# Media attention with turns four groups behind the scores, and fixed parts of the eight banks

## What is computed

```python
def _L2_xattn_ref(x, media, media_mask, ...):
    qn = layernorm(x, ln_q_g, ln_q_b)
    q = qn @ Wq * scale
    k, v = jnp.split(media @ Wkv, 2, axis=-1)
    sim = jnp.einsum('bhid,bhjd->bhij', q, k)
    sim = jnp.where(media_mask[:, None, None, :], sim, neg_inf)
    attn = jax.nn.softmax(sim, axis=-1)
    out = jnp.einsum('bhij,bhjd->bhid', attn, v)
    x = x + jnp.tanh(attn_gate) * (out @ Wo)
    h = gelu(layernorm(x, ...) @ W1) @ W2
    return x + jnp.tanh(ff_gate) * h
```

## Time and profile before

| | us |
|---|---|
| median of 3 executions | 1693.32 (1692.87 to 1697.88) |
| the profiled execution | 1686.46 |
| its span, first to last instruction | 1684.4 |
| PE busy | 1552.4 (92%) |
| PE weight loads busy | 1339.0 (79%) |
| DVE busy | 967.5 (57%) |
| ACT busy | 668.8 (40%) |
| mean granted clock of PE | 0.968 of full speed |

### The profile page before, as it was taken

The page is one execution under the profiler, slowest core; times in us unless marked ns, Lnnn a source line. Parts: engine busy times, 40 slices in busy tenths (PEclk is TensorE's granted clock), DMA queues, the critical chain, the costliest instruction groups (busy, mean ns, idle before and its releaser), DMA issues.

```text
span 1684.4 us, 31094 instructions
## 1 busy us (share of the span) xinstructions
PE 1552.4 (92%) x11106; PEld 1339.0 (79%) x11106; DVE 967.5 (57%) x2163; ACT 668.8 (40%) x1773; POOL 246.7 (15%) x346
## 2 busy tenths in 40 slices
PE   5879899899899899999889999998999999899899
PEld 4747677667667679999778878887988878788799
DVE  2646655646646675676274646564655555647554
ACT  1314334434424462222454444443336353535332
POOL 0134324324324300000000000000100000000010
PEclk9989999999999889999999999999999999999999
DMA  3203000000000020000100000002000000000000
GB/s 144 69 13 107 4 1 3 3 0 3 3 0 1 1 82 1 0 0 1 53 5 4 3 3 3 1 1 82 0 33 25 4 3 3 3 0 1 1 25 26
DMA packets 13224, 30.20 MB, mean 18 GB/s; under 512 B 2400, under 2 KB 8800, under 8 KB 12512
## 3 DMA queue, kind: packets, MB, share of 16 engines
q1 hardware_dynamic: 13152, 29.23, 4.9%
HBM read 27.13 MB, written 2.10 MB: 17 GB/s over the span
## 4 chain that ended last, share of the span: by engine, by line
PE 77%; DVE 10%; issue 6%; ACT 3%; POOL 2%; DMA 0%; DVEq 0%; SPq 0%; ACTq 0%; POOLq 0%
PE bank L774 69%; PE bank L787 8%; DVE nmax L1258 2%; DVE pT L1157 2%; DVE stats L1187 1%; ACT p L1472 1%; DVE xn L1233 1%; POOL kbd L1652 1%; DVE xn L1237 1%; POOL rstd L1619 1%; DVE o_rounded L1342 0%; ACT hT L1423 0%; DVE aggr L1192 0%; DVE xn L1235 0%; DMA p<-in_media 0%
## 5 line engine op out<-in xcount | busy, mean ns | idle before, releaser
L1472 ACT ACTIVATE p<-bank,nmax 128x128 f32<-128x128 f32 x1024 | 285.4, 375 | 394.3 <-DVE nmax L1258 393.9
L774 PE MATMUL bank<-v,pT 128*128 128x65 f32 (+2 forms) x2048 | 258.1, 263 | 46.1 <-issue 25.0
L774 PEld LDWEIGHTS bank<-v,pT 128*128 128x128 f32 x2048 | 252.3, 194 | 54.0 <-issue 42.3
L1258 DVE TENSOR_REDUCE nmax<-bank 128x4 f32<-128x512 f32 x256 | 170.1, 686 | 161.7 <-PE bank L774 161.4
L774 PE MATMUL bank<-w_ff_rounded,hT_rounded 128*128 128x256 f32 x944 | 218.4, 287 | 0.8 <-DVE kbd L1320 0.8
L774 PE MATMUL bank<-kbd,hT 64*128 64x128 f32 (+1 forms) x1280 | 205.1, 342 | 5.0 <-ACT hT L1423 3.9
L787 PEld LDWEIGHTS bank<-consts,p 128*128 128x128 f32 x1040 | 125.4, 143 | 100.4 <-issue 79.5
L774 PE MATMUL bank<-xT_rounded,w_ff_rounded 128*128 128x256 f32 x864 | 196.8, 286 | 4.5 <-issue 3.0
L1157 DVE COPY pT<-bank 128x512 f32<-128x512 f32 x256 | 174.6, 682 | 34.8 <-PE bank L787 34.3
L774 PE MATMUL bank<-xn_rounded,w_ff_rounded 128*128 128x256 f32 x608 | 172.9, 284 | 0.0
L787 PE MATMUL bank<-consts,p 128*128 128x128 f32 x1040 | 161.6, 278 | 7.5 <-ACT p L1432 5.0
(11 more groups left out here) (147 smaller groups left out, 2798.8 us busy)
## 6 DMA issues: line engine op xcount, KB each, us to landing
ctxT<-in_ctxT SPq DMA_DIRECT2D x32, 128.0 KB, 2.4
w_ff<-in_w1b SPq DMA_DIRECT2D x6, 640.0 KB, 6.6
w_att<-in_w2a SPq DMA_DIRECT2D x1, 3072.0 KB, 10.6
w_att<-in_w3a SPq DMA_DIRECT2D x1, 3072.0 KB, 10.3
w_att<-in_w1a SPq DMA_DIRECT2D x1, 2432.0 KB, 12.3
hT<-in_xT SPq DMA_DIRECT2D x8, 256.0 KB, 3.1
o<-in_x SPq DMA_DIRECT2D x8, 256.0 KB, 3.1
w_ff<-in_w2b SPq DMA_DIRECT2D x1, 2048.0 KB, 7.4
```

The costliest lines, as they stand in the source:

```text
L774: return pe.matmul(dst, lhsT, rhs, start=first, stop=last)
L1258: dve.tensor_reduce(nmax[:, ph.place[s] % P_RING, :], bank[:, :].rearrange("p (h t) -> p h t", h=QUAD), AX_X, ALU.max, negate=True).then_i ...
L1472: t = act.activation(p_ring[i % P_RING][:, part], bank[:, part], ACT.Exp, bias=nmax[:, i % P_RING, j:j + 1])
```

## The change

In media attention the turn moves from two groups behind the scores to four, and the product from three to five. An iteration has 21 slots instead of 19. There are eight `p` buffers there instead of four; the new four lie in free columns of `kbd0` and `kbd1`. Banks are no longer dealt over all steps in phases 3 and 5: scores use banks 0 to 3 in turn, every `oT2` uses bank 7, and all other steps share banks 4 to 6 in turn. In `steps_attn2` unit A's four `oT2` go to slots 8, 9, 11 and 12, its `wo` to slot 15, B's `oT2` to slots 17 to 20, and the third `oT2_low` of B is put ahead of B's last `oT2`. No instruction that computes is added or removed. The other phases keep their order and banks. Lines of the changed kernel stand 3 to 18 lower: matmuls at L792, transposes at L805, DVE's maxima at L1276, its copy of a turn at L1175, its low part at L1360.

```diff
+MEDIA_RING = 8
+MEDIA_SKEW_T = 4
+MEDIA_SKEW_O = 5
...
-        if 0 <= i - SKEW_T < len(groups):
-            slot += here(("turn",) + groups[i - SKEW_T])
-        if 0 <= i - SKEW_O < len(groups):
-            slot += here(("values",) + groups[i - SKEW_O])
+        if 0 <= i - skew_t < len(groups):
+            slot += here(("turn",) + groups[i - skew_t])
+        if 0 <= i - skew_o < len(groups):
+            slot += here(("values",) + groups[i - skew_o])
...
-                 (a, n, n + SKEW_O),
-                 (low(A_), n + 1, n + SKEW_O + 1),
-                 (here(("wo", A_), ("end", A_)), n + SKEW_O + 2, n + SKEW_O + 2),
+                 (a, n, n + skew_o),
+                 (low(A_), n + 1, n + skew_o + 1),
+                 (here(("wo", A_), ("end", A_)), n + skew_o + 2, n + skew_o + 2),
...
+                 (low(B_)[2:3], end, end),
                  (b[3:], end, end),
                  (ahead(*pre[-2:]), end, end),
-                 (low(B_)[2:], end, end),
+                 (low(B_)[3:], end, end),
...
         self.bank = {s: i % BANKS for i, s in enumerate(jobs)}
+        if index in (3, 5):
+
+            of_scores = [s for s in jobs if s[0] == "scores"]
+            others = [s for s in jobs if s[0] not in ("scores", "oT2")]
+            self.bank = {s: i % QUAD for i, s in enumerate(of_scores)}
+            self.bank |= {s: QUAD + i % (QUAD - 1) for i, s in enumerate(others)}
+            self.bank |= {s: BANKS - 1 for s in jobs if s[0] == "oT2"}
...
+        p_media = [p[:, :] for p in p_ring] + [kbd[u][:, at:at + BANK] for at in (2304, 2816) for u in range(UNITS)]
```

More of the change, by code:

```diff
@@ L114, in ahead, with attention @@
     return [(s, 1) for s in steps]
-def attention(streams):
+def attention(streams, skew_t, skew_o):
     groups = [(kind, u, b, g) for kind, u in streams for b in range(ROWS) for g in range(GROUPS)]
     slots = []
-    for i in range(len(groups) + SKEW_O):
+    for i in range(len(groups) + skew_o):
         slot = []
@@ L201, in steps_self @@
     end = 4 * n + SKEW_O - 1
-    return weave(attention([("self", A_), ("self", B_), ("cross", A_), ("cross", B_)]),
+    return weave(attention([("self", A_), ("self", B_), ("cross", A_), ("cross", B_)], SKEW_T, SKEW_O),
                  (here(*pre_self(B_)[2:]), 0, n - 1),
@@ L240, in steps_attn2 @@
     n = ROWS * GROUPS
-    end = 2 * n + SKEW_O - 1
+    skew_o = MEDIA_SKEW_O
+    end = 2 * n + skew_o - 1
     a, b = (here(*[("oT2", u, b, j) for b in range(ROWS) for j in range(2)]) for u in range(UNITS))
-    return weave(attention([("media", A_), ("media", B_)]),
+    return weave(attention([("media", A_), ("media", B_)], MEDIA_SKEW_T, skew_o),
                  (here(*pre_attn2(B_)), 0, n - 2),
-                 (a, n, n + SKEW_O),
-                 (low(A_), n + 1, n + SKEW_O + 1),
-                 (here(("wo", A_), ("end", A_)), n + SKEW_O + 2, n + SKEW_O + 2),
+                 (a, n, n + skew_o),
+                 (low(A_), n + 1, n + skew_o + 1),
+                 (here(("wo", A_), ("end", A_)), n + skew_o + 2, n + skew_o + 2),
                  (ahead(*norms), n, n + 3),
@@ L250, in steps_attn2 @@
                  (low(B_)[0:2], end - 2, end - 1),
-                 (ahead(*pre[:-3]), n + SKEW_O + 1, end - 1),
+                 (ahead(*pre[:-3]), n + skew_o + 1, end - 1),
                  (ahead(*pre[-3:-2]), end, end),
+                 (low(B_)[2:3], end, end),
                  (b[3:], end, end),
                  (ahead(*pre[-2:]), end, end),
-                 (low(B_)[2:], end, end),
+                 (low(B_)[3:], end, end),
                  (here(("wo", B_), ("end", B_)), end, end))
@@ L459, in build @@
         pT_ring = [sb_twin(f"pT{i}", [P, BANK]) for i in range(PT_RING)]
-        nmax = sb("nmax", [P, P_RING, QUAD])
+        nmax = sb("nmax", [P, MEDIA_RING, QUAD])
         rinv = sb("rinv", [P, 2, QUAD])
@@ L574, in x_low, with ring @@
             return xn[u][:, c, 1, :]
+        p_media = [p[:, :] for p in p_ring] + [kbd[u][:, at:at + BANK] for at in (2304, 2816) for u in range(UNITS)]
+        def ring(ph, s):
+            return ph.place[("scores",) + s[1:]] % (MEDIA_RING if s[1] == "media" else P_RING)
         def head_width(kind):
@@ L907, in turn_p @@
                 pe.wait_ge(*after(ph, it, ("scores",) + s[1:], "exp"))
-                turn(s, ph.bank[s], [p_ring[ph.place[s] % P_RING][:, j * P:(j + 1) * P] for j in range(QUAD)])
+                turn(s, ph.bank[s], [p_media[ring(ph, s)][:, j * P:(j + 1) * P] for j in range(QUAD)])
             def values(ph, it, s, bank):
@@ L1257, in scores @@
                 dve.wait_ge(*after(ph, it, s, "mm"))
-                dve.tensor_reduce(nmax[:, ph.place[s] % P_RING, :], bank[:, :].rearrange("p (h t) -> p h t", h=QUAD),
+                dve.tensor_reduce(nmax[:, ring(ph, s), :], bank[:, :].rearrange("p (h t) -> p h t", h=QUAD),
                                        AX_X, ALU.max, negate=True).then_inc(sems[s[0], "max"], 1)
@@ L1464, in scores @@
             def scores(ph, it, s, bank):
-                i = ph.place[s]
+                i = ring(ph, s)
                 act.wait_ge(*after(ph, it, s, "max"))
-                before, back = ph.earlier(("turn",) + s[1:], P_RING)
+                before, back = ph.earlier(("turn",) + s[1:], MEDIA_RING if s[1] == "media" else P_RING)
                 act.wait_ge(*after(ph, it, before, "copied", back))
@@ L1471, in scores @@
                     part = slice(j * P, (j + 1) * P)
-                    t = act.activation(p_ring[i % P_RING][:, part], bank[:, part], ACT.Exp,
-                                       bias=nmax[:, i % P_RING, j:j + 1])
+                    t = act.activation(p_media[i][:, part], bank[:, part], ACT.Exp,
+                                       bias=nmax[:, i, j:j + 1])
                 t.then_inc(sems[s[0], "exp"], 1)
```

## The result

| | before | after |
|---|---|---|
| median, us | 1693.12 (1692.87 to 1697.88, 4 runs) | 1768.49 (1765.40 to 1771.61, 4 runs) |
| profiled execution, us | 1686.46 | 1767.46 |
| its span, us | 1684.4 | 1765.4 |
| mean granted clock of PE | 0.968 | 0.955 |

The change makes the kernel slower: ratio 1.0438, 95% interval 1.0412 to 1.0465, or 75 us between the medians and 81 us between the two profiled executions. The forecast was 1754 (1722 to 1788).

A forecast was written before the change was run, and what follows sets the result against it. PE, busy 92% of the span, was taken as the bound, so only its waits count: +41 (six loop iterations), +10 (two written-out ones), +10 (clock) on 1686.5, plus 6.9 to the median, gave 1754 us (1722 to 1788).

The forecast's parts named there:

- head: `k2` for ACT's scaling, `v2` for the key copy: Start of a media iteration: `k2` waits 1.8 us for the bank of `nT2`, `v2` 1.1 us for the first `k2`'s.
- slot 9, second `oT2`: In bank 7 the second `oT2` waits 2.1 us for the first one's low part on DVE.
- slots 11 and 12: Third and fourth `oT2` wait 3.1 us together for low parts and, for the fourth, unit A's last normalization.
- slots 18 and 19: Each `oT2` of unit B waits 1.5 us for a low part queued behind a product's normalization on DVE.
- waits gone: Old PE waits per loop iteration, at the head and slots 11 and 13 (3.0, 0.9, 1.2 us): 5.1 us replaced.
- The fourth iterations: The two written-out media iterations: slots 9 to 12 and the tail add 4.9 us each, +10 together.
- The preparation before the loop: New preparation step in three banks: no cost, as two steps of 0.86 us cover a copy of 0.7.
- The clock: PE's clock falls behind waits: 0.21 us lost per us waited, so +10 us for another 50 us of waits.
- every wait brings a fall of the clock: Rival: 1.6 us for each of some four more waits per iteration, +44 instead of +10, 1787 us; chance 12%.
- The skew: Longer skew and more p buffers: no gain, since exponentials are not what PE waits for in the loop.
- faster rival: Longer skew lets PE run ahead of DVE, so waits for copies and clock losses go: 1648 us; chance 5%.
- The two rules: Skill rules: more `p` buffers would remove the head's 2.82 us wait; a single `oT2` bank should lose, unpriced.

The follow-up runs named there:

- `banks_alone`: The changed kernel with turn and product back at two and three groups behind, fixed banks kept: 1783.49 us, ratio 1.0517 to the kernel before.
- `skew_alone`: The changed kernel with banks dealt in turn over all steps in every phase, longer skew and eight p buffers kept: 1682.06 us, ratio 0.9932.
- `low_at_once`: The changed kernel with each `oT2_low` in the slot of its own transpose instead of one slot later: 1739.25 us, ratio 1.0263.
- `low_part_later`: The kernel before with the low part of unit B's `nT2` as its own step ahead of the fourth `k2`: 1663.60 us, ratio 0.9814.
- `low_and_norm_later`: `low_part_later` with unit B's two norm steps moved from slots 10 to 12 into slots 14 and 15: 1655.26 us, ratio 0.9774.

## Why the prediction was right, and which terms were off

The table sets its terms against the trace of the changed kernel, the loop iteration at 1399.12. Waits are counted as there, from the moment at which PE could have started, by the distance from start to start less the usual one.

| term, us per loop iteration | forecast | measured |
|---|---|---|
| head: `k2` for ACT's scaling, `v2` for the key copy | 1.8, 1.1 | 1.96, 1.02 |
| slot 9, second `oT2` | 2.1 | 2.36 |
| slots 11 and 12 | 3.1 | 2.64, in slot 12 |
| slot 15, `wo` | 0.8 | 0.51 |
| slots 18 and 19 | 1.5, 1.5 | 1.50, 1.50 |
| sum | 11.9 | 11.5 |
| waits gone | 5.1 | 5.0 |

**Bank 7 and the head** came out as worked out. `banks_alone` and `skew_alone` show that the fixed parts are the cause, the lists of waits that it is the single bank in the main, `low_at_once` that DVE's order makes up a large part of it, `low_part_later` that the head's "issue" was DVE's queue behind the low part of `nT2`. In slots 11 and 12 the two waits came as one: in the iteration shown slot 11's transpose started at 970.65, when the low part it needs had ended at 969.68. Counted over all six loop iterations the waits grew from 32.2 to 70.4 us, +38 against the +41 of the sum.

**The fourth iterations** were forecast at +4.9 each in waits. They measure about +7 each (12.5 to 19.7 and 12.5 to 19.5). What the working had missed are turns behind `wo`, which in three banks wait for the adding to `x_all` and for normalizations, as PE shows it in phase 3:

```profile
1166.13 0.66 PE L805 MATMUL bank<-consts,kbd 128*128 128x128 f32 x4 [0.84 <-DVE x_all L1388]
1168.36 0.66 PE L805 MATMUL bank<-consts,kbd 128*128 128x128 f32 x4 [0.73 <-DVE o L1290]
```

**The preparation before the loop** was costed at nothing, on the ground that two steps of 0.86 cover a copy. It costs some 2.4 us in each phase. For phase 3 only its waits show it (three for `v`, 2.2 us): the start of that phase by itself moves by as much, from 832.4 us in `skew_alone` to 838.6 in `low_part_later`. At the start of phase 5 keys wait for copies of values on ACT:

```profile
1287.79 1.13 PE L792 MATMUL bank<-ctxT,w_att 128*128 128x256 f32 x4 [1.05 <-ACT v L1441]
1290.47 1.13 PE L792 MATMUL bank<-ctxT,w_att 128*128 128x256 f32 x4 [0.69 <-ACT v L1441]
```

**The clock** is the term that was off most: +10 forecast, about +24 between the two profiled executions. The two levels of the clock and the mean of a span give the time at the lower one: 2 x (1 - 0.968) x 1684.4 = 108 us before, 2 x (1 - 0.955) x 1765.4 = 159 after. Within the eight media iterations the clock record of the trace shows it grow from 37.5 to 85.3 us, and a piece at half speed loses half of that time if PE works all through it: +24, an estimate. Nearly the same comes from the other side. The eight iterations grew by 76 us together (637.0 to 713.1), and 52 of these are waits (38 and 14). The step that was wrong took 0.21 us lost per us waited, from falls behind the head's wait alone, and applied it to waits at other places. Measured is 24 for 52, 0.46 per us. In the worst case, the fourth iteration of phase 5, the clock stands at 0.85 for 92 us.

Of these 24 some are chance. The clock differs between executions of one kernel: of nine executions of the kernel before beside `low_and_norm_later`, the fastest took 1684.64 us at a mean of 0.968 and the slowest 1707.62 at 0.955. The profiled execution of before has 0.968 and lies 6.7 us under its median, that of the change lies 1.0 under its own. By the medians 75 less 57 of waits leave 18 for the clock, 0.35 per us waited.

So of the 81 us between the profiled executions, 52 are waits (forecast 51), 24 the clock (10) and 5 the starts of phases (0). The forecast of +61 was 20 low, by the last two. Part of that was made up by luck: the 6.9 us that were added for the distance of the median from the profiled execution are only 1.0 in the changed kernel, and so 1754 is only 14 off. The rival "every wait brings a fall of the clock" (+44, where 1.6 for four waits in six to eight iterations is 38 to 51) went too far by 20; the first two loop windows above, with 10.7 and 11.5 us of waits, stand at 0.94 and 0.98.

**The skew**, costed at no gain, is worth 11 us with dealt banks. Exponentials were not what PE waited for, but at the head a longer skew puts keys and values where a turn and a product were, and PE has them to do while DVE is held up. Its waits there fall from 3.0 to about 1.6 us, as `skew_alone` shows:

```profile
922.57 0.39 PE L792 MATMUL bank<-kbd,share 64*128 64x512 bf16 x2 [0.61 <-DVE kbd L1338]
924.95 0.48 PE L792 MATMUL bank<-ctxT,w_att 128*128 128x256 f32 x1 [0.38 <-ACT p L1490]
```

That is not all gained: behind unit A's last product a transpose now waits 1.0 to 2.3 us for `o`, so that an iteration has 3.8 to 5.0 us of waits against 5.0. Between the profiled executions the eight media iterations give 6.0 us, and 3.0 more lie ahead of phase 3, which the edit leaves alone. How the 11 us of the medians come about is thus shown in part only. The prediction's faster rival named this mechanism with 1648; its bound (bank waits above 5.1 us per iteration) held, and with the banks dealt it is 1682.

**The two rules.** The changed kernel has eight `p` buffers and still loses 3.0 us at the head; `low_part_later` has four and loses nothing. The hint of the Trainium skill (Perfetto Trace Analysis, Optimization Strategy), that the same gap repeating can mean too few buffers, doesn't hold for this gap. The 62.4 us of waits at a bank that all output transposes share, against 2.5 with dealt banks, are this case's price for what the Trainium skill (Perfetto Trace Analysis, Optimizing Tensor Performance) says without one: independent groups of matmuls should rotate through banks.

What stays open is why the same wait brings a fall of the clock in one iteration and none in the next; no run was made for it. No run gives output transposes two banks and leaves the other parts alone either, so what the three shared banks cost by themselves stays an estimate from the waits for `xn`, `v` and `kbd`.

## What to carry to other kernels

A fixed part of the banks for one kind of work is only as good as the slowest emptying of its few banks; here the emptying is done by an instruction that stands several places down in another engine's list, so look at that list before giving a kind of work one bank. If PE waits for "issue", ask what the engine that should release it is itself waiting for: one DVE instruction, queued too early behind ACT, held up a copy, and moving it brought 30 us with no new buffer or bank. And price a wait by more than its own length where waits bring the clock down.

## What was not expected of the hardware

Waits of 1.5 to 2.6 us, five in an iteration of 88 us, go with a lower granted clock for PE more often than one of 3.0 and two of about 1 us did before. Within the six loop iterations of media attention the clock was at 1.2 GHz for 17 us before and 44 us after. The mean over a span was 0.968 before (0.955 to 0.968 in other executions of it), 0.955 after and 0.941 in `banks_alone`, which is 108, 159 and 210 us at 1.2 GHz, while PE's busy time with the same 11106 matmuls was 1552.4, 1586.0 and 1600.2 us. And in `low_part_later` all six loop iterations, left with two waits of about 1 us each, stand at 1.00, while its two fourth iterations hold 20.5 us each at 1.2 GHz, more than the 13.7 and 6.8 before: the falls came elsewhere, and why is open.
